# First pass over a quantised block moved from ScalarE to VectorE, the matmul wait split per bank, one semaphore per slot of x, and new work orders

## The reference, cut to what matters

```
def act_quant(x):                 # per token
    scale = 127.0 / clip(max(abs(x), axis=-1), 1e-5)
    return clip(round(x * scale), -128, 127) / scale
def bitlinear(x, w): return einsum('bsi,oi->bso', act_quant(x), weight_quant(w))
def ffn(x):                       # 512 -> 2048 -> 512
    gate = silu(bitlinear(x, w_gate)); up = bitlinear(x, w_up)
    return bitlinear(gate * up, w_down)
x = x + tanh(g_xattn) * attention(layernorm(x), ctx, 16 heads, 77 keys, mask)
x = x + tanh(g_ffn) * ffn(layernorm(x))
```

## Time and profile before

| | |
|---|---|
| profiled execution | 1431.91 us |
| its span, first to last instruction | 1430.1 us |
| TensorE | busy 1290.9 us, 90% |
| VectorE | busy 1082.1 us, 76% |
| ScalarE | busy 985.8 us, 69% |
| GpSimd | busy 726.9 us, 51% |
| mean granted TensorE clock | 0.973 |

### The profile page before, as it was taken

How to read it: one execution, slowest core, us unless ns; L and a number is a source line. 1 busy time by engine, 2 the same in 40 slices (tenths; PEclk the granted TensorE clock), 3 DMA queues, 4 the chain that set the end, 5 groups by cost and what they waited for, 6 DMA issues and landing times.

```text
span 1430.1 us, 25966 instructions
## 1 busy us (share of the span) xinstructions
PE 1290.9 (90%) x7424; PEld 618.0 (43%) x7744; DVE 1082.1 (76%) x2577; ACT 985.8 (69%) x1404; POOL 726.9 (51%) x1187
## 2 busy tenths in 40 slices
...
GB/s 279 228 214 133 61 114 136 123 129 116 123 139 110 128 118 147 99 130 115 125 125 118 140 108 128 123 125 128 105 147 115 136 105 135 114 123 113 70 82 74
DMA packets 386616, 181.63 MB, mean 127 GB/s; under 512 B 324147, under 2 KB 357811, under 8 KB 384947
## 3 DMA queue, kind: packets, MB, share of 16 engines
...
...
## 4 chain that ended last, share of the span: by engine, by line
PE 45%; DVE 27%; ACT 9%; issue 9%; POOL 4%; DMA 4%; SPq 1%; POOLq 0%; ACTq 0%; DVEq 0%
PE bank L1198 17%; PE bank L1210 7%; DVE nmax L954 5%; PE bank L1070 5%; PE bank L1072 5%; PE bank L1071 5%; DVE xh L944 3%; PE bank L1143 3%; DVE region L1015 3%; ACT work L710 2%; DVE o L1039 2%; DVE xn L939 2%; ACT work L711 2%; DVE st L986 2%; ACT region L742 2%
## 5 line engine op out<-in xcount | busy, mean ns | idle before, releaser
L610 POOL TENSOR_TENSOR region<-region,up 128x512 f32<-128x512 f32 x256 | 331.2, 1299 | 305.5 <-DVE region L1015 168.3
L1198 PE MATMUL bank<-tern_gate,region 128*128 128x512 fp8e4 x1024 | 266.3, 383 | 26.6 <-ACT up L750 12.8
L1198 PE MATMUL bank<-tern_up,region 128*128 128x512 fp8e4 x1024 | 264.8, 381 | 0.0
L1015 DVE SCALAR_TENSOR_TENSOR region<-region,bank 128x512 f32<-128x512 f32 x256 | 172.7, 679 | 116.3 <-ACT region L742 116.1
L1210 PE MATMUL bank<-tern_down,region 128*128 128x512 fp8e4 x1024 | 233.9, 382 | 13.0 <-DMA region<-hb 7.0
L742 ACT ACTIVATE region<-bank,fs 128x512 f32<-128x512 f32 x256 | 177.7, 694 | 65.9 <-PE bank L1198 65.3
L601 POOL TENSOR_TENSOR work<-work 124x512 f16<-124x512 f32 x160 | 195.8, 1232 | 49.0 <-ACT work L711 48.1
L750 ACT ACTIVATE up<-bank 128x512 f32<-128x512 f32 x256 | 154.3, 604 | 59.5 <-PE bank L1198 46.8
L1021 DVE TENSOR_REDUCE hmx<-region 128x1 f32<-128x512 f32 x256 | 168.9, 676 | 5.7 <-POOL region L610 5.7
L754 ACT ACTIVATE region<-region,fs 128x2048 f32<-128x2048 f32 x64 | 127.9, 1999 | 48.9 <-DVE fs L1032 48.9
L1198 PEld LDWEIGHTS bank<-tern_up,region 128*128 128x128 bf16 x1024 | 100.8, 98 | 122.7 <-issue 3.3
(11 more groups left out here) (141 smaller groups left out, 2341.3 us busy)
## 6 DMA issues: line engine op xcount, KB each, us to landing
...
```

Of the source, the lines that this page charges most:

```text
L610: nc.gpsimd.tensor_tensor(ht, ht, up[:, n % 2, :], ALU.mult).then_inc(hmul_ready, 1)
L1015: V.scalar_tensor_tensor(ht, ht, 1.0, pb[2 * (n % 2)][:, :], ALU.add, ALU.mult).then_inc(silu_ready, 1)
L1198: ins = T.matmul(pb[2 * (n % 2) + w][:, :], xqT[:, k, tok], tern[w][:, k * FF + n * GT:k * FF + (n + 1) * GT], start=(k == 0), stop=(k == ...
```

## The change

1. `hq` is taken from ScalarE and written on VectorE, same data in place.
2. In `F:gu` on TensorE the wait for `up_ready` stands between the gate and the up matmuls, with a second extra weight load.
3. `up_copy` waits for `hmul_ready` also in the first two quarters of a block, unless it is group 0.
4. `x_in` becomes three semaphores, one a slot, and the loads no longer wait for one another.
5. `masks` is cut in two: clearing the scalars (`W:hc`) and the rest (`W:hd`).
6. All lists of all engines are new.

```
-                    pe.wait_ge(up_ready, f * (TT * FN) + (at - 1))
...
                 T.ldweights(xqT[:, 0, tok], tile_position=(0, 0))
                 for w in range(2):
+                    if w == 1 and (at >= 2 or not first(f)):
+                        pe.wait_ge(up_ready, f * (TT * FN) + (at - 1))
+                        T.ldweights(xqT[:, 0, tok], tile_position=(0, 0))
...
-            def hq(f, t, _):
-                act.wait_ge(hscale_ready, f * TT + (t + 1))
-                nc.scalar.activation(h[:, t % 2, :], h[:, t % 2, :], ACT.Copy, bias=MAGIC,
-                                     scale=fs[:, t, HSC:HSC + 1]).then_inc(hq_ready, 1)
...
+            def hq(f, t, _):
+                dve.wait_ge(hscale_ready, f * TT + (t + 1))
+                V.tensor_scalar(h[:, t % 2, :], h[:, t % 2, :], fs[:, t, HSC:HSC + 1], MAGIC, ALU.mult, ALU.add).then_inc(hq_ready, 1)
...
-                dve.wait_ge(x_in, g * 16 + 16)
+                dve.wait_ge(x_in[g % 3], g // 3 * 16 + 16)
```

```
 TENSOR_ORDER = """
-    F:gu00 A:sc00 A:sc01 F:gu01 A:sc02 A:sc03 A:sc04 F:gu02 A:sc10 F:gu03 A:pv00 A:pv01 A:sc11 A:pv02 F:gu10
-    A:sc12 E:down30 A:sc13 A:sc14 A:pv03 F:gu11 F:gu12 A:pv10 A:pv11 F:gu13 F:gu20 A:pv12 A:pv13 A:wo00 A:wo10
-    F:down00 A:wo20 F:gu21 F:gu22 F:gu23 Q:q00 Q:q10 Q:q20 Q:q30 A:wo30 Q:s00 F:gu30 Q:s01 F:down10 Q:s10 Q:s11
-    Q:s20 Q:s21 F:gu31 Q:s30 F:gu32 Q:s31 F:gu33 Q:mT00 F:down20
+    F:gu00 F:gu01 F:gu02 F:gu03 A:sc00 A:sc01 F:gu10 A:sc02 E:down30 A:sc03 A:sc04 F:gu11 A:sc10 F:gu12 A:sc11
+    A:pv00 F:gu13 A:pv01 A:sc12 A:sc13 A:pv02 F:gu20 A:sc14 A:pv03 F:down00 A:pv10 A:pv11 F:gu21 A:pv12 A:pv13
+    F:gu22 A:wo00 A:wo10 F:gu23 Q:q00 Q:q10 Q:q20 Q:q30 A:wo20 Q:s00 F:gu30 Q:s01 F:down10 Q:s10 A:wo30 Q:s11
+    F:gu31 Q:s20 F:gu32 Q:s21 F:gu33 Q:s30 Q:s31 F:down20 Q:mT00
 SCALAR_ORDER = """
+    F:gu00 F:up00 F:gu01 F:up01 E:hb30 F:gu02 F:gu03 F:up02 A:sc00 F:gu10 A:sc01 F:up03 A:sc02 F:up10 A:sc03
...
 VECTOR_ORDER = """
+    F:gu00 E:hq30 F:gu01 F:hm00 F:hm01 F:gu02 F:gu03 F:gu10 E:down30 F:hm02 F:hm03 F:hs00 F:gu11 F:hq00 F:gu12
...
+    A:wo00 A:st00 F:hm13 F:hm20 F:hs10 A:wo10 A:al12 A:zn00 A:za00 F:gu22 Q:q00 A:st10 Q:q10 F:hq10 A:zn10
+    F:hm21 F:gu23 F:hm22 A:za10 F:hm23 Q:q20 Q:q30 F:hs20 Q:s00 A:al13 A:wo20 Q:s01 F:gu30 A:st20 F:hq20 Q:s10
+    F:down10 A:zn20 A:za20 A:wo30 Q:s11 A:st30 Q:s20 F:gu31 F:gu32 Q:s21 A:zn30 F:gu33 Q:s30 F:hm30 F:hm31 Q:s31
+    A:za30 Q:mh00 F:hm32 F:down20 F:hm33 F:hs30
```

More of the change, by code:

```diff
@@ L72 @@
+    N:xh00 A:ah03 F:up13 N:xh10 F:gu20 F:up20 A:ah10 F:up21 N:xh20 F:gu21 A:ah11 F:up22 F:gu22 N:xh30 A:ah12
+    Q:q00 F:gu23 F:up23 A:zq00 Q:q10 A:ah13 F:hb10 Q:q20 Q:q30 A:zq10 A:zb00 A:zb10 F:gu30 F:hb20 F:up30 F:gu31
+    A:zq20 A:zb20 F:gu32 F:up31 F:up32 F:gu33 F:up33 A:zq30 Q:mT00 A:zb30
 """
 VECTOR_ORDER = """
[L74 to L75 removed]
@@ L91 @@
+    A:tz20 F:down10 A:kv10 Q:qs10 A:vl40 Q:kv00 F:down20 Q:m00 A:tz30
 """
@@ L130 @@
-    A:sc12 E:down30 A:sc13 A:sc14 A:pv03 F:gu11 F:gu12 A:pv10 A:pv11 F:gu13 A:pv12 A:pv13 F:gu20 A:wo00 F:down00
-    A:wo10 F:gu21 F:gu22 F:gu23 F:gu30 F:down10 A:wo20 F:gu31 F:gu32 F:gu33 A:wo30 F:down20 G:gu00 G:gu01 G:gu02
-    G:gu03 G:gu10 H:down30 G:gu11 G:gu12 G:gu13 G:gu20 G:down00 G:gu21 G:gu22 G:gu23 G:down10 G:gu30 G:gu31
+    A:sc00 F:gu00 A:sc01 F:gu01 F:gu02 F:gu03 A:sc02 A:sc03 E:down30 A:sc04 A:sc10 F:gu10 F:gu11 A:sc11 F:gu12
+    A:pv00 A:sc12 A:pv01 F:gu13 A:sc13 F:gu20 A:sc14 A:pv02 F:down00 A:pv03 A:pv10 F:gu21 F:gu22 F:gu23 F:gu30
@@ L133 @@
+    A:pv11 F:down10 A:wo00 F:gu31 A:pv12 A:pv13 F:gu32 F:gu33 A:wo10 F:down20 G:gu00 G:gu01 G:gu02 G:gu03 A:wo20
+    H:down30 G:gu10 G:gu11 G:gu12 G:gu13 A:wo30 G:down00 G:gu20 G:gu21 G:gu22 G:gu23 G:down10 G:gu30 G:gu31
     G:gu32 G:gu33 G:down20 I:down30
@@ L135 @@
 SCALAR_LAST = """
-    E:hq30 A:sc00 A:sc01 A:sc02 F:gu00 F:up00 A:sc03 F:gu01 A:sc04 F:up01 E:hb30 F:gu02 F:up02 A:ah00 F:gu03
-    A:sc10 F:gu10 A:sc11 A:ah01 F:up03 F:up10 A:sc12 A:sc13 A:ah02 A:sc14 F:gu11 F:up11 A:ah03 F:gu12 F:hq00
-    A:ah10 F:hb00 F:up12 A:ah11 F:up13 F:gu13 F:up20 A:ah12 F:gu20 F:hq10 A:ah13 F:hb10 F:gu21 F:gu22 F:up21
-    F:up22 F:gu23 F:up23 F:up30 F:gu30 F:hq20 F:hb20 F:gu31 F:up31 F:gu32 F:up32 F:gu33 F:up33 A:zq00 A:zq10
-    A:zb00 A:zb10 H:hq30 H:hb30 G:gu00 G:up00 A:zq20 G:gu01 G:up01 G:gu02 G:up02 G:gu03 G:up03 A:zb20 G:gu10
@@ L141 @@
-    G:up10 G:hq00 G:hb00 G:gu11 G:up11 G:gu12 A:zq30 G:up12 G:gu13 G:up13 G:gu20 G:up20 A:zb30 G:hq10 G:hb10
-    G:gu21 G:up21 G:gu22 G:up22 G:gu23 G:up23 G:hq20 G:gu30 G:up30 G:gu31 G:up31 G:gu32 G:up32 G:gu33 G:up33
-    G:hb20 I:hq30 I:hb30
+    A:sc00 F:gu00 F:up00 E:hb30 F:gu01 F:up01 F:gu02 A:sc01 F:gu03 A:sc02 F:up02 A:sc03 F:up03 A:sc04 A:sc10
+    F:gu10 F:gu11 F:up10 F:up11 A:sc11 F:gu12 F:hb00 A:ah00 F:gu13 F:up12 F:up13 A:sc12 A:sc13 A:ah01 F:up20
+    A:sc14 A:ah02 F:gu20 F:hb10 F:gu21 F:up21 F:gu22 A:ah03 F:up22 F:gu23 F:up23 F:gu30 A:ah10 F:up30 F:hb20
```

126 lines of the change are left out of this document (59 added, 67 removed).

## The result

| | before | after |
|---|---|---|
| median of the runs | 1431.88 us (4 runs, 1428.67 to 1435.95) | 1476.97 us (4 runs, 1472.8 to 1478.48) |
| ratio, 95% interval | | 1.0309 [1.0275, 1.0342] |
| span of the profiled execution | 1430.1 us | 1475.1 us |
| busy: TensorE, VectorE, ScalarE, GpSimd | | 1309.9, 1212.5, 859.5, 750.5 us |

A forecast was written before the change was run, and what follows sets the result against it. TensorE was taken to bound the loops: 75 us dense plus 3.2 lost is 78.2 a loop against 81.54, 46 us less over 14; front 0, end -3, giving 1383 us, with 1350 to 1424 to hold 8 in 10.

The forecast's parts named there:

- the price of a loop's first half: First half of each loop, where scores, exponentials and GpSimd run close behind each other: 1.0 us of loss added.
- the 1.63 assumed: hq on VectorE, sometimes blocked by GpSimd: 1.63 us each, between 1.28 and 2.55, 6.5 us a loop.
- The split wait: Gate products on TensorE no longer wait for the up copy: up to 12.8 us in all, 0.9 a loop.
- Extra loads: 256 extra weight loads on TensorE: 0.01 us each, 0.2 us a loop, at most 0.1 each.
- E:down30 without slack: Down matmuls starting at 10.1 us of a loop may wait for their transposed block; rival of 1457 us, chance 0.10.
- VectorE behind wo00: From 38.8 us of a loop, VectorE has 37.2 us of work against TensorE's 36.2; 2.0 us of loss taken.
- if score pairs still stand in gaps: Sign in the changed profile's loops: score pairs still standing in gaps would show the prediction wrong.
- The maxima's copy through SP: Issued behind down20's store at about 78.8 us, landing 1 us before the next loop's first scores: no cost.
- The front: Part ahead of the loops, a chain through all engines: 0 us of change, between -8 and +8.
- The end: Part behind the loops, with down20 starting some 4 us earlier: -3 us, between -7 and +3.
- the last tile's chain then decides: In the end, scale, hq, hb, DMA and down set the time: gains 0.7 and up to 2.4, loses some 1 us.
- VectorE becomes the bound: Rival: VectorE takes the loops' gain, each hq at 2.55 us instead of 1.63; 1428 us, chance 0.18.

The follow-up runs named there:

- e6: Changed kernel with GpSimd's subtraction for the probabilities' low half cut from 512 to 16 columns in all blocks but the first (output differs): 1390.1 us.
- e9: Changed kernel with GpSimd's 512-column subtraction replaced by five 16-column pieces in all blocks but the first (output differs): 1402.3 us.
- e10: Changed kernel with VectorE's low-half subtractions al and xl written as scalar_tensor_tensor instead of tensor_tensor: 1478.6 us.
- e11: Changed kernel with VectorE's al and xl subtractions and the normalisations xn and zn all written as scalar_tensor_tensor: 1490.5 us.
- e4: Kernel before with only the wait for up_ready moved between gate and up matmuls, with its second extra weight load: 1427.4 us.
- e5: Changed kernel with, in the loops alone, VectorE's output of down00 moved ahead of pv03 and hq back on ScalarE: 1466.4 us.
- e7: Kernel before with GpSimd's subtraction for the probabilities' low half cut from 512 to 16 columns in all blocks but the first (output differs): 1442.0 us.

## Why the prediction was wrong

**The step that failed** is the price of a loop's first half: "I add 1.0 us for the first half, where scores, exponentials and GpSimd run close behind each other". Its VectorE steps were not laid out one by one, as those behind wo00 were. The prediction saw the hold in the earlier trace rows, on a zn, and charged it to hq alone; hq itself was hardly held, 1.33 us against the 1.63 assumed. But the new order also put xn and al beside GpSimd's subtractions, and these rose by 0.37 us x 4 and 0.34 us x 8 a loop, 4.2 us (xl, which fell from 0.88 to 0.69 us, gave back 0.19 x 4 = 0.8). Several of them stand in a row ahead of the output that frees TensorE's bank, so TensorE waited, and then ran at half clock. In the loop shown, the ten us from 947 to 957 hold 3.94 us of TensorE's idle time, and 2.35 us of slower matmuls go with them: 6.3 us where 1.0 was added. Over the loops it is 84.6 measured against 78.2 forecast.

**What held of the sum.** With GpSimd's long subtractions gone the loop measured 78.6 us in e6, which has less work to do, and 79.5 in e9, where GpSimd's time is nearly kept. So the rest of the sum comes out 0.4 to 1.3 us short a loop; that e6 comes so close to 78.2 is in part luck, since e6 leaves work out. With all the work done no order here came under 80.9.

The Trainium skill (SBUF — State Buffer, section Who interferes with whom) says more than the sentence that the prediction took from it: a VectorE instruction with two SBUF inputs also contends with a GpSimd one that reads SBUF. The trace agrees: al, 128x256 with both inputs in SBUF, went to 1.51 us, and in e10 and e11 the scalar_tensor_tensor with both inputs in SBUF is held too. The rule was there; I read it for the step that the change is about and not for those that the new order moved.

Point by point:
- The split wait: the waits are gone as said; worth 0.3 us a loop in e4, inside "up to 0.9". Extra loads: nothing that shows, as said.
- E:down30 without slack: TensorE waits for a transposed block four times in the whole kernel, 7.9 us, and 6.24 of them in the last down of all; that rival fell.
- VectorE behind wo00, said to be 1 us late: TensorE's waits for the maxima are 28.3 us in all, 43 of them, none over 1.3, so 2.0 us a loop, and this term of 2.0 came true (before: 15.2 us). It is also the sign "if score pairs still stand in gaps" by which the prediction said it would be wrong. The large loss stood in the other half.
- The maxima's copy through SP: in time in the loops, late by 4.38 us in the last part, where scores stand first; with the two half quarters at half clock behind it that is most of the end's loss. I hadn't laid that list out.
- The front: +0.65 us, within -8 to +8. The end: -3 forecast, +5.4 measured. Of its two terms the first came true, in that down20 waits 1.04 us instead of 6.21 and runs dense. But the last down, dense before, now has the same stall, as "the last tile's chain then decides" had feared, and none of the gain was left: from the last up matmuls to the end it is 21.21 us (1453.89 to 1475.1), against 21.07 before.

```profile
1465.82 5.94 PE L1210 MATMUL bank<-tern_down,region 128*128 128x512 fp8e4 x16 [6.24 <-DMA region<-hb]
```

- The rival "VectorE becomes the bound" named the right mechanism, but its bound of 1428 took the hold for hq only. No case held a late VectorE step followed by TensorE's half clock, and the price of the clock was nowhere in the sum, although two loops of before show it: the granted clock was 0.50 from 718 to 720 us and 0.66 from 1126 to 1130, and these loops took 83.22 and 82.84 us, the other twelve 81.5 to 82.2.

What stays open: why e5's two edits undo each other, why e7 is 0.6% slower than the kernel before, and what the waits would cost without the half clock, since no run has the one without the other.
